# Attention maxima in pieces of at most 512 columns, three one-bank slots, scores through three banks

## The reference

```python
q, k, v = jnp.split(jnp.einsum('bsd,de->bse', x, W_qkv), 3, axis=-1)
q = _layernorm(q, q_scale); k = _layernorm(k, k_scale)   # then reshaped to (B, S, H=16, Hd=8)
scores = jnp.einsum('bshd,bthd->bhst', q / jnp.sqrt(Hd), k)
scores = jnp.where(future[None, None], jnp.finfo(scores.dtype).min, scores)
attn = jax.nn.softmax(scores, axis=-1)
ctx = jnp.einsum('bhst,bthd->bshd', attn, v)
out = jnp.einsum('bsd,de->bse', ctx.reshape(B, S, D), W_out)
```

## Time and profile before

| | us |
|---|---|
| median of 3 runs | 3990.48 (3989.49 to 3993.26) |
| the profiled execution | 3989.54 |
| its span, first to last instruction | 3987.8 |
| mean granted TensorE clock | 0.973 of full |

### The profile page before, as it was taken

One profiled execution on the slowest core, in us unless ns is written; L12 is line 12 of the kernel. 1 busy time (PEld: TensorE's weight loads), 2 busy tenths in 40 slices (PEclk: granted clock), 3 DMA queues, 4 the chain that ended last, 5 costly groups with the idle time before them and its releaser, 6 DMA issues. The chain is left out here.

```text
span 3987.8 us, 172955 instructions
## 1 busy us (share of the span) xinstructions
PE 3691.3 (93%) x65553; PEld 2532.0 (63%) x65792; DVE 3204.8 (80%) x6126; ACT 2905.2 (73%) x5873; POOL 3061.3 (77%) x3927
## 2 busy tenths in 40 slices
PE   4788888589999999999999999999999999999997
PEld 2333434257777777777777777777777777777775
DVE  7676666278888888888888888888888888888885
ACT  5465656467777777777777777777777777777775
POOL 4111111289999999999999999999999999999994
PEclk7799899799999999999999999999999999999999
DMA  2422220122222322222322223222232222222222
GB/s 80 69 37 33 29 30 9 50 73 66 66 64 66 92 63 63 63 63 69 85 63 63 63 64 93 65 65 66 64 91 63 63 63 63 74 65 65 66 65 58
DMA packets 176123, 250.55 MB, mean 63 GB/s; under 512 B 46726, under 2 KB 65796, under 8 KB 175108
## 3 DMA queue, kind: packets, MB, share of 16 engines
q1 hardware_dynamic: 176004, 248.94, 25.5%
HBM read 39.08 MB, written 8.39 MB: 12 GB/s over the span
## 5 line engine op out<-in xcount | busy, mean ns | idle before, releaser
L1041 PE MATMUL w_ring<-w_wqkv,w_xs 128*128 (+1 forms) x2304 | 1157.1, 605 | 24.7 <-DMA w_scales<-in_L_ffn_k_scale 19.8
L1432 POOL TENSOR_TENSOR w_qr<-w_raw,w_tc 128x512 f32<-128x512 f32 x384 | 488.9, 1273 | 174.6 <-PE w_ring L1061 168.2
L1446 POOL TENSOR_TENSOR w_qr<-w_qr,w_qrot 128x512 f32<-128x512 f32 x384 | 572.1, 1490 | 0.0
L1041 PEld LDWEIGHTS w_ring<-w_wqkv,w_xs 128*128 128x128 f32 x2304 | 379.4, 191 | 190.8 <-issue 163.0
L637 DVE TENSOR_REDUCE a_row_max<-a_ring 128x1 f32<-128x640 f32 (+6 forms) x352 | 353.3, 1028 | 178.7 <-PE a_ring L467 172.6
L1439 POOL TENSOR_TENSOR w_qrot<-w_raw,w_tc 128x512 f32<-128x512 f32 x384 | 485.8, 1276 | 0.0
L607 POOL TENSOR_SCALAR_AFFINE_SELECT a_probs<-a_probs 128x512 f32<-128x512 f32 x128 | 81.2, 634 | 502.0 <-ACT a_probs L572 502.0
L572 ACT ACTIVATE a_probs<-a_wide 128x512 f32<-128x512 f32 (+1 forms) x608 | 323.4, 573 | 184.2 <-PE a_wide L488 112.2
L1117 PEld LDWEIGHTS w_ring<-w_pts,w_vw 64*64 64x64 f32 x24576 | 376.7, 135 | 92.9 <-issue 92.9
L1232 ACT ACTIVATE w_ksq<-w_ring 128x512 f32<-128x512 f32 x384 | 229.3, 597 | 271.4 <-PE w_ring L1041 271.4
L1117 PE MATMUL w_ring<-w_pts,w_vw 64*64 64x32 f32 x24576 | 398.3, 220 | 4.2 <-issue 2.4
(11 more groups left out here) (157 smaller groups left out, 8551.7 us busy)
## 6 DMA issues: line engine op xcount, KB each, us to landing
w_vw<-w_v SPq DMA_DIRECT2D x1152, 128.0 KB, 2.3
w_vw<-w_v SPq DMA_DIRECT2D x768, 64.0 KB, 2.0
a_q_stack<-q_parts SPq DMA_DIRECT2D x144, 64.0 KB
a_k_stack<-k_parts SPq DMA_DIRECT2D x144, 64.0 KB
w_wqkv<-in_L_ffn_Wqkv SPq DMA_DIRECT2D x6, 1536.0 KB, 6.0
q_parts<-ap_parts SPq DMA_DIRECT2D x8, 384.0 KB, 3.5
k_parts<-ap_parts SPq DMA_DIRECT2D x8, 384.0 KB, 3.5
w_wo<-in_L_ffn_Wo SPq DMA_DIRECT2D x12, 256.0 KB, 3.4
```

Source lines behind the costliest of these rows:

```text
L1041: nc.tensor.matmul(bank(what, i, u)[:], xs[u][:], rhs, start=True, stop=True).then_inc(done, 1)
L1432: nc.gpsimd.tensor_tensor(by_head(qr[i][:]), by_head(raw[i][:]), wide(table(u, Q_COS)), ALU.mult).then_inc(q_straight[i], 1)
L1446: nc.gpsimd.tensor_tensor(qr[i][:], qr[i][:], qrot[i][:], ALU.add).then_inc(q_added[i], 1)
```

## The change

- `ring` is three slots of one bank (512 columns) in place of two of two banks; `wide_bank` is three banks in place of two. With `out_bank` this is again all of PSUM.
- A maxima piece has at most 512 columns: 38 of them in a step. The later blocks of queries (c = 4 to 7) are cut at key 512; the maxima of the second parts go to `row_max2`, and one more DVE instruction joins them before the splitting. PE's matmuls stay the same in number and size; their order within a block c changes.
- PE may fill a slot when the piece three before it is read, and likewise for the score banks.
- `turn_context`, `turn_tokens` and `project`, with the DVE instructions behind them, come in halves of four blocks of 128 tokens. They stand at pieces 11 and 12, 16 and 17, 22 and 23; `turn_maxima` stands at piece 3. Counted by blocks c, these are the places of before.
- The order of maxima and scores is worked out anew from the costs of the new pieces. A step on PE now reads M0 M1 M2 [V7, turn_maxima] M3 M4 M5 s0 M6 s1 M7 s2 M8 s3 M9 s4 M10 s5 s6 M11 s7 M12 s8 M13 s9 M14 s10 M15 s11 M16 s12 s13 M17 s14 M18 s15 V0, s16 M19 s17 M20 s18 M21 s19 M22 s20 M23 s21 V1, M24 s22 s23 M25 s24 M26 s25 M27 s26 V2, M28 M29 s27 s28 M30 s29 M31 s30 V3, M32 s31 M33 s32 s33 M34 s34 V4, M35 s35 M36 s36 V5, M37 s37 V6.

```diff
+        row_max2 = sb("row_max2", [P, AG, S // P - 4])
-        ring = [ctx.enter_context(nc.psum_tensor(f"a_ring{n}", [P, S], F32)) for n in range(2)]
-        wide_bank = [ctx.enter_context(nc.psum_tensor(f"a_wide{n}", [P, 512], F32)) for n in range(2)]
+        ring = [ctx.enter_context(nc.psum_tensor(f"a_ring{n}", [P, 512], F32)) for n in range(3)]
+        wide_bank = [ctx.enter_context(nc.psum_tensor(f"a_wide{n}", [P, 512], F32)) for n in range(3)]
...
-        max_units = [(h, n, c) for c, n in ((0, 4), (1, 4), (2, 2), (3, 2), (4, 1), (5, 1), (6, 1), (7, 1)) for h in range(0, AG, n)]
+        max_units = []
+        for c in range(KC):
+            for k0 in range(0, (c + 1) * P, 512):
+                k1 = min(k0 + 512, (c + 1) * P)
+                n = min(AG, 512 // (k1 - k0))
+                max_units += [(h, n, c, k0, k1) for h in range(0, AG, n)]
...
+        MAX_AT, CTX_AT, TOK_AT, PROJECT_AT = 3, 11, 16, 22
...
+        def same_bank_before(w):
+            return w - 3 if w >= 3 else max(v for v in range(NS) if v % 3 == w) - NS
...
             def maxima(b, hg, n):
-                wait(pe, r_done, ring_at(b, hg, n) - 1)
-                if n == 3 and parts_of(alike(b, hg))[1]:
+                h0, heads, c, k0, k1 = max_units[n]
+                wait(pe, r_done, ring_at(b, hg, n) - 2)
+                if n == MAX_AT + 1 and parts_of(alike(b, hg))[1]:
                     wait(pe, placed_act, 2 * GROUPS * b + 2 * hg)
...
+                    mm = nc.tensor.matmul(bank[:, at:at + width], q_stack[hg][0:96, h0 + i, c * P:(c + 1) * P],
+                                          k_stack[hg][0:96, h0 + i, k0:k1], start=True, stop=True)
+                    if k1 == (c + 1) * P:
+                        mm = nc.tensor.matmul(bank[:, at + width - P:at + width], ident_bf[:], mask_qk[:], start=False, stop=True,
+                                              skip_group_check=True)
...
-                wait(pe, exp_done, n2 * NS + (w - 1))
+                wait(pe, exp_done, n2 * NS + (same_bank_before(w) + 1))
...
-            def project(b, hg):
-                wait(pe, r_done, ring_at(b, hg, PROJECT) - 1)
-                wait(pe, r_done, ring_at(b, hg, TURN_TOK) + 1)
-                for c in range(KC):
+            def project(b, hg, j):
+                wait(pe, r_done, ring_at(b, hg, PROJECT[j]) - 2)
+                wait(pe, r_done, ring_at(b, hg, TURN_TOK[j]) + 1)
+                for c in range(KC // 2):
...
+                linked(nc.vector.tensor_tensor(row_max[:, :, 4:KC], row_max[:, :, 4:KC], row_max2[:], ALU.max))
                 linked(nc.vector.tensor_scalar(part[0], row_max[:], -1.0, None, ALU.mult))
...
-            def normalise(b, hg):
+            def normalise(b, hg, j):
                 dve.sem_clear(link)
-                wait(dve, r_done, ring_at(b, hg, TURN_CTX))
-                wait(dve, r_full, ring_at(b, hg, TURN_CTX) + 1)
+                wait(dve, r_done, ring_at(b, hg, TURN_CTX[j]))
+                wait(dve, r_full, ring_at(b, hg, TURN_CTX[j]) + 1)
+                blocks = slice(KC // 2 * j, KC // 2 * (j + 1))
```

More of the change, by code:

```diff
@@ L382, in uses_of @@
             for n in range(NMAX):
-                out += [TURN_MAX] * (n == 2 and has_scores) + [TURN_CTX] * (n == 6 and has_ctx)
-                out += [TURN_TOK] * (n == 10 and has_batch) + [PROJECT] * (n == 14 and has_batch) + [n] * has_max
+                out += [TURN_MAX] * (n == MAX_AT and has_scores)
+                for j in range(2):
+                    out += [TURN_CTX[j]] * (n == CTX_AT + j and has_ctx)
+                    out += [TURN_TOK[j]] * (n == TOK_AT + j and has_batch) + [PROJECT[j]] * (n == PROJECT_AT + j and has_batch)
+                out += [n] * has_max
             return out
@@ L547, in step @@
                                 turn_maxima(b, hg)
[L548 to L553, removed]
+                        for j in range(2):
+                            if n == CTX_AT + j and has_ctx:
+                                turn_context(b, hg, j)
+                            if n == TOK_AT + j and has_batch:
+                                turn_tokens(b, hg, j)
+                            if n == PROJECT_AT + j and has_batch:
+                                project(b, hg, j)
                         if has_max:
@@ L576, in place_maxima @@
                 wait(act, r_full, ring_at(b, hg, TURN_MAX) + 1)
-                bank = slot(b, hg, TURN_MAX)[:, 0:512].bitcast(BF16)
+                bank = slot(b, hg, TURN_MAX)[:].bitcast(BF16)
                 for hh in range(2, AG):
@@ L674, in normalise @@
                 dve.wait_ge(link, 1)
                 before = (hg - 2) % GROUPS
-                out = ctx_tok[:, :, AG * AHD * before:AG * AHD * (before + 1)]
+                out = ctx_tok[:, blocks, AG * AHD * before:AG * AHD * (before + 1)]
                 nc.vector.tensor_tensor(out.rearrange("p c (h d) -> p c h d", h=AG), bank[:, :, :, 0:AHD],
[L678 to L682, removed]
@@ L684, in add_projection, with copy_turned @@
[L684 to L687 removed]
+                                        inv[:, blocks, :].unsqueeze(3).broadcast_to([P, KC // 2, AG, AHD]), ALU.mult).then_inc(r_done, 1)
+            def copy_turned(b, hg, j):
+                wait(dve, r_full, ring_at(b, hg, TURN_TOK[j]) + 1)
+                nc.vector.tensor_copy(ctx_f[:, 512 * j:512 * (j + 1)], slot(b, hg, TURN_TOK[j])[:]).then_inc(r_done, 1)
@@ L689, in step, with add_projection @@
+            def add_projection(b, hg, j):
+                wait(dve, r_full, ring_at(b, hg, PROJECT[j]) + 1)
+                chunk = t.xtok[:, bass.ds((b - 1) * KC + KC // 2 * j, KC // 2), :].rearrange("p c d -> p (c d)")
+                nc.vector.tensor_tensor(chunk, slot(b, hg, PROJECT[j])[:], chunk, ALU.add).then_inc(r_done, 1)
             def step(b, hg):
```

78 lines of the change are left out of this document (36 added, 42 removed).

## The result

The changed kernel takes 3942.74 us (median of 3 runs, 3937.6 to 3943.08) against 3990.48: a ratio of 0.9876, 95% interval 0.9862 to 0.989. That is 47.7 us less; 35.6 were forecast, and the time lies in the range given. The profiled execution took 3937.6 us with a span of 3935.9; it is the fastest of the three.

What follows compares the result with a forecast made beforehand. PE, DVE and ACT were taken to wait for each other in turn through few slots. 13 steps at 2.2 us, two at 1.0, 3.0 and 2.0 at the end: 35.6 us less, 3955 us, range 3933 to 3979.

Steps and rivals of the forecast that it cites:

- more than forecast: Rival: V0 comes at PE's own pace and the clock drops less, 3.2 us a step, 3937 us; chance 0.09.
- the turn: End of a step, from V7 through ACT's context and placing copies to PE's restart: 0, bounds -0.5 and 0.3 us.
- DVE's added cost: Per step, 16 more reductions 1.0 us, joining maximum 0.25, halved `normalise` 0.4: 1.65 us more, 26.7 busy.
- Stretch (a): From PE's restart behind the placing copies to V0, 10.14 us: DVE sets the pace, gain 0.8 us a step.
- Stretch (c): From V3 to V7: moved maxima pieces cost 0.2 us and give 0.2, so 0, bounds -0.5 and 0.3.
- The two steps of the loop's turning back: Two of 15 intervals, where PE stands 4.66 us, then runs at half clock: gain 1.0 us each.
- First step: Maxima alone, 27.9 us, DVE busy 24.65: added DVE work against smaller idle pieces, 0, bounds -0.5 and +1.5 us.
- Steps 16 and 17: The end: 3.0 us from the third score bank in step 16, 2.0 from overlapping projection halves in step 17.
- The clock: Sign of a wrong forecast: a PE clock in the body below 0.93; it stood at 0.95 before.
- the bank gives nothing: Rival: ACT still waits for values of two blocks earlier, so banked scores lie idle; 14 us gained, 3976; chance 0.20.
- DVE becomes the bound: Rival: each extra reduction costs 148 ns, V0 comes later and the ring runs dry; slower, 4010 us; chance 0.08.
- Nothing changes by more than 0.2%: Rival: the ring's smaller depth takes what the bank gives, change within 8 us; chance 0.07.

Runs made afterwards that it cites:

- the extra reductions: The changed kernel with DVE reducing pieces 7 to 10 twice, 2.4 us more DVE work ahead of V0: 3969.91 us, ratio 0.9947.
- the small pieces alone: The kernel before with only the 38 pieces of at most 512 columns, two two-bank ring slots, two score banks, turns and projection whole: 4032.73 us, ratio 1.011.
- The busy PE: The changed kernel with PE making the first matmul of M3 nine times instead of once while it waits for the placing copies: 3926.75 us, ratio 0.9839.

## Why the prediction was right, and where its sizes were off

The mechanism of the forecast is what the runs show: take the third score bank away and the gain is gone. By the stages of the two profiles 46.3 us are gained, 10.7 more than forecast: 4.0 of them in the body's intervals, 1.9 in the first step and 4.8 in the last two steps, where the clock was no term of the sum. The time is near the 3937 of "more than forecast", but not by its way: V0 didn't reach PE's own pace, and the body's clock fell.

- **What bounds the kernel**: right. PE stood for score banks and DVE had slack. The time went where it was put: 2.4 us of a step at full clock, of which 1.08 before V0, 1.31 in the three gaps behind V0 to V2, 0.1 from V3 to V7 and 0 in the turn (in the loop's steps 0.9, 1.3, 0.1 and 0). Forecast were 0.8, 1.2, 0 and 0, and 0.2 beside them.
- **DVE's added cost**: 1.65 us forecast, 1.4 measured (25.0 to 26.4 busy). The fixed part of 0.06 us for one more reduction held: seven in a row go at 0.60 each. The 125 ns of the Trainium skill, Perfetto Trace Analysis, Optimizing Scalar/DVE Operations, would have made it an estimated 2.0 us for the reductions alone; the trace does not agree, with 1.4 us for all of it, and the measurement decides. The joining maximum took 0.17 us (0.25 taken), the halves of `normalise` 2 x 0.55 (1.3 taken, with the chains).
- **Stretch (a), "paced by DVE"**: right after the change, by the extra reductions: 2.4 us for 2.4. From the end of DVE's placing to V0 the working gave 9.3 us, and it is 9.3 (173.30 to 182.62); its 185.8 on the way should read 185.7. But the working gave the gain before V0 to the ring and the pieces. Of the 0.91 us that V0 gains in the loop (10.16 to 9.25), 0.64 are the bank's: with two it comes at 9.89. The step that failed is the sentence that ACT's exponentials do not delay V0. They ended in time, but with two banks each score waits for the exponential two before: PE's loads wait 2.5 us for ACT in this stretch before, 2.8 with two banks after, and 0.4 with three. The stretch waited for DVE and ACT in turn.
- **Stretch (c), taken as 0**: right as a sum, by luck in part. V3 to V4 gave 0.38 us where 0.2 was allowed, and by the two-bank kernel all of it is the bank's; the maxima that moved behind V4 cost 0.56 there where 0.2 was allowed, and V5 to V6 gave 0.26 that was not in the account.
- **The two steps of the loop's turning back**: 1.0 us each forecast, 1.5 and -0.3 measured. The clock is down for 13.7 us at each turning back in both kernels, and PE waits 4.16 and 3.2 us for nothing that is shown. The second of these steps now also has 6.8 us at half clock ahead of V0, which it had not before. The two steps behind them gained 3.1 and 2.4 us.
- **First step, 0 forecast**: 1.9 us gained. DVE is busy 24.6 us in both; before, it went through its 22 pieces in 24.1 us with 1.45 us of idle time in five places, now through 38 in 21.8 without any:

```profile
113.10 21.83 DVE L653 TENSOR_REDUCE a_row_max<-a_ring 128x4 f32<-128x512 f32 x38 [9.40 <-PE a_ring L480]
```

  The clock of that stretch was also higher, 0.57 in place of 0.50; as DVE never waited in it for PE, that gave nothing.
- **Steps 16 and 17, 5.0 forecast**: 9.8 measured, and what is mis-sized is not the bank but the clock, which the sum put at nothing. Up to the last copy of the context it is 32.7 us before and 27.5 now. The three kernels with two score banks and 6.8 us at half clock in this stretch take 31.9 to 32.3, those with three and also 6.8 us 28.4 to 28.7: 3.2 to 3.8 us for the bank, 3.0 forecast. From that copy on it is 12.05 us before and 7.43 now. With 6.8 us at half clock it takes 11.3 with the projection whole (the small pieces alone) and 9.6 with its halves: 1.7 us for these, 2.0 forecast. The other 4 to 5 us go with the clock: 20.7 us at half clock in these two steps before, 3.4 now. The matmuls of the projection took 3.75 us and take 2.0.
- **The clock**: not in the sum, though named as a sign. The body's clock fell from 0.95 to 0.94: 12 half-clock stretches in place of 8, of which nine in place of five begin at the turn. PE now stands 1.84 us for the placing copies where it stood 1.08; behind the turned maxima it has one product and its mask to issue (M3) in place of two of each. The busy PE shows the price: 16 us.
- **The rivals**: "the bank gives nothing" is refuted the hard way: without it the change is worth nothing (1.0003). "DVE becomes the bound" came true in one stretch only, and V0 came sooner there, not later. That two slots measure 4005.64, near the 4010 of this rival, is chance: the rival had three slots and 148 ns a reduction, and the reductions kept to 0.60 us. "Nothing changes by more than 0.2%", the smaller depth taking what the bank gives, is refuted by 47.7 us.
- **The windowed part**: the 5.6 us of the profile are no gain that is shown; between the medians the change is worth 47.7.

## What to carry to other kernels

An extra buffer is worth what its producer waits for it in all stretches; look at each of them, also at those in which another engine seems to set the pace. Smaller pieces can be a loss with the same number of slots (43 us here) and still be right, when they free the memory for more slots and for the buffer that matters. When PE gets faster and then stands at a fixed chain of other engines, look at its clock behind that place: here 1.3 us of repeated work there in each step gave 16 us in all. Before calling the forecast for a stage right or wrong, compare the clock of that stage in both profiles: the last two steps ran 20.7 us at half clock before and 3.4 after.

## What was not expected of the hardware

- Steps of one kernel that differ only in a 3.4 us stretch at half clock take 32.6 to 32.8 or 34.0 us, 1.2 to 1.4 more; the stretches begin at the turn, where PE stands 1.84 us, from 0.6 us ahead of its restart to 1.4 behind it.
- PE work that computes nothing new made the kernel 16 us faster, from 0.94 to 0.98 of the granted clock.
- Where a loop turns back, PE stands 4.16 and 3.2 us without a cause in the profile and goes 13.7 us at half clock; with the loop written out both are gone, and the step takes 33.9 us in place of about 41.
- The same windowed part takes 3233 to 3246 us in the profiles of these kernels.
